# Expert layers: turning X for the router by transposing DMAs in place of TensorE

## The reference

```python
x = x + _L0_ffn_ref(_layernorm(x, axis=-1), L0_ffn_w_router, L0_ffn_w1, L0_ffn_w2, L0_ffn_bias)
# in it, with xf the 2048 tokens x 256 and 8 experts:
scores = jax.nn.softmax(xf @ w_router, axis=-1)
expert_weights, top_experts = jax.lax.top_k(scores, TOP_K)   # TOP_K = 2, capacity 512 per expert
...
x = x + _L1_ffn_ref(_layernorm(x, axis=-1), L1_ffn_W1, L1_ffn_b1, L1_ffn_W2, L1_ffn_b2, L1_ffn_Wr, L1_ffn_br)
# in it:
logits = xf @ Wr + br
topv, _ = lax.top_k(logits, TOPK)
```

## Time and profile before

| | us |
|---|---|
| median of 2 runs | 2664.79 |
| their range | 2664.3 to 2665.28 |
| the profiled execution, span from first to last instruction | 2672.0 |
| what lies outside that span | not listed |

### The profile page before, as it was taken

The page is one execution under the profiler, slowest core; times in us unless marked ns, Lnnn a source line. Parts: engine busy times, 40 slices in busy tenths (PEclk is TensorE's granted clock), DMA queues, the critical chain, the costliest instruction groups (busy, mean ns, idle before and its releaser), DMA issues. The chain is left out here.

```text
span 2672.0 us, 46118 instructions
## 1 busy us (share of the span) xinstructions
PE 2419.7 (91%) x14931; PEld 1416.2 (53%) x15058; DVE 1908.5 (71%) x3499; ACT 1673.2 (63%) x2692; POOL 1804.4 (68%) x1581
## 2 busy tenths in 40 slices
PE   6999999999999999999997588879999999678886
PEld 3555555555555555555553467645444444467665
DVE  7878777787777877777775655468888898764332
ACT  4556756557665566656664555458888788576453
POOL 2677867777777777776768455436878789355553
PEclk9999999999999999999999799989999999699998
DMA  4000000000000000000000744430202020573223
GB/s 144 1 1 1 25 1 1 1 1 5 22 1 1 1 1 1 1 1 1 1 1 15 193 112 116 92 97 18 57 17 58 2 49 1 165 202 72 35 39 60
DMA packets 90917, 107.85 MB, mean 40 GB/s; under 512 B 18867, under 2 KB 80260, under 8 KB 90708
## 3 DMA queue, kind: packets, MB, share of 16 engines
q1 hardware_dynamic: 68500, 80.57, 10.1%
q0 software_dynamic: 21696, 24.98, 6.1%
q10 hardware_dynamic: 544, 0.00, 0.0%
HBM read 68.75 MB, written 25.88 MB: 35 GB/s over the span
## 5 line engine op out<-in xcount | busy, mean ns | idle before, releaser
L417 POOL TENSOR_TENSOR a_acc<-a_acc,a_pf 128x512 f32<-128x512 f32 (+1 forms) x480 | 650.9, 1356 | 312.4 <-ACT a_pf L574 290.7
L574 ACT ACTIVATE a_pf<-a_psS 128x1024 f32<-128x1024 f32 (+1 forms) x288 | 281.5, 977 | 306.1 <-PE a_psS L717 301.8
L869 DVE TENSOR_TENSOR a_pl<-a_pf,a_ph 128x512 f16<-128x512 f32 x448 | 438.2, 988 | 23.2 <-ACT a_ph L580 23.0
L2161 POOL TENSOR_TENSOR c_pl<-c_pf,c_ph 128x512 f16<-128x512 f32 x320 | 374.9, 1199 | 116.9 <-ACT c_ph L2260 116.5
L845 DVE TENSOR_REDUCE a_mx<-a_psA 128x1 f32<-128x512 f32 x504 | 335.3, 683 | 43.7 <-PE a_psA L652 39.6
L580 ACT ACTIVATE a_ph<-a_psS 128x1024 f16<-128x1024 f32 (+1 forms) x288 | 281.5, 977 | 0.0
L1417 POOL DMA_INDIRECT f_sums<-f_xn,f_sidx x78 | 140.5, 1801 | 208.1 <-DVE f_xn L1815 185.6
L1261 DVE TENSOR_TENSOR f_xn<-f_xn 128x256 f16<-128x256 f32 x312 | 130.5, 424 | 197.8 <-ACT f_xn L1230 175.3
L2493 DVE TENSOR_REDUCE c_wf<-c_psA 128x1 f32<-128x512 f32 x384 | 246.5, 681 | 20.1 <-PE c_psA L2332 19.9
L1148 PE MATMUL f_psH<-f_xh,f_w 128*128 128x256 f16 x624 | 173.4, 278 | 83.3 <-ACT f_xn L1230 68.2
L2253 ACT ACTIVATE c_pf<-c_psS 128x1024 f32<-128x1024 f32 x192 | 197.9, 1030 | 67.1 <-PE c_psS L2366 66.0
(11 more groups left out here) (364 smaller groups left out, 6382.0 us busy)
## 6 DMA issues: line engine op xcount, KB each, us to landing
f_stage<-in_L_ffn_w SPq DMA_DIRECT2D x16, 1024.0 KB
f_stage<-in_L_ffn_W SPq DMA_DIRECT2D x16, 1024.0 KB
c_kst<-c_khs SPq DMA_DIRECT2D x64, 100.1 KB, 2.2
a_cx<-in_ctx SPq DMA_DIRECT2D x4, 1536.0 KB
c_cx<-in_ctx SPq DMA_DIRECT2D x12, 512.0 KB, 4.0
f_sums<-X SPq DMA_DIRECT2D x2, 2048.0 KB, 13.2
f_xrow<-f_xn SPq DMA_DIRECT2D x8, 512.0 KB, 4.4
c_kst<-c_kls SPq DMA_DIRECT2D x32, 100.1 KB, 2.2
```

What stands on the lines that cost most here:

```text
L417: g.tensor_tensor(acc[0:k, p, :], acc[0:k, p, :], pf[0:k, q % RF, i, :], ALU.add).then_inc(s_acc, 1)
L574: act.activation(pf[0:r, q % RF, 0:k, :], psS[q % 2][0:r, 0:k, :], ACT.Exp, scale=SCALE).then_inc(s_pF, 1)
L869: v.tensor_tensor(pl[0:r, q % RP, i, :], pf[0:r, q % RF, i, :], ph[0:r, q % RP, i, :], ALU.subtract).then_inc(s_pL, 1)
L2161: g.tensor_tensor(pl[0:r, q % RP, i, :], pf[0:r, q % RF, i, :], ph[0:r, q % RP, i, :], ALU.subtract).then_inc(s_pG, 1)
```

## The change

ScalarE makes the high halves of X in X's own layout, four pieces of 128 x 1024 into `xrh`, and DVE the low halves into `xrl` (`row_low`). Both lie in the space of the weights of expert E - 2. SP then issues eight transposing DMAs, `dma_start_transpose`, each of which turns 128 x 1024 float16 (eight blocks of 128 x 128) into `xth` or `xtl`. In SP's list they stand after the small loads and ahead of the weights of expert 0, of the copies of X and of the rows of `xn`, each behind a wait for its own half. TensorE's transposes of X, ScalarE's and DVE's reads of PSUM and the semaphores between them go. The router's matmuls wait once, for all eight transfers. On DVE the new `row_low` steps take places among the statistics; in layer 1, the branch with `early_stats is None`, the last of them stands ahead of `means(1)`.

```diff
--- before.py
+++ after.py
@@ -953,7 +953,6 @@
              1: ("L1_ffn_Wr", "L1_ffn_W1", "L1_ffn_W2")}[layer]
     GELU = ACT.Gelu_apprx_tanh if layer == 0 else ACT.Gelu
     NQ = NT // 4
-    GI = KC * NQ
     PR = ring(FT, 4)
     HR = ring(FT, 3)
     PIECES = FT
@@ -977,7 +976,8 @@
 
 
         late = w16[:, E - 1, :, :].rearrange("p a f -> p (a f)").bitcast(F32)
-        xth, xtl = w16[:, E - 1, 0:2, :], w16[:, E - 1, 2:4, :]
+        xth, xtl = (w16[:, E - 1, a:a + 2, :].rearrange("p a (t c) -> p (a t) c", c=P) for a in (0, 2))
+        xrh, xrl = (w16[:, E - 2, a:a + 2, :].rearrange("p a f -> p (a f)") for a in (0, 2))
         wb = late.rearrange("p (t c) -> p t c", c=D)
         xn = sb("xn", [P, NT, D])
 
@@ -1050,7 +1050,6 @@
         psH = [ctx.enter_context(nc.psum_tensor(tag + f"psH{i}", [P, 512], F32)) for i in range(3)]
         psX = ctx.enter_context(nc.psum_tensor(tag + "psX", [P, 512], F32))
         psY = [ctx.enter_context(nc.psum_tensor(tag + f"psY{i}", [P, 512], F32)) for i in range(2 * IT)]
-        ring4 = psH + [psX]
         psR = psY[2][:, 0:(NT + 1) * E].rearrange("p (t e) -> p t e", e=E)
         psI = psY[0][:, 0:HI]
         psC = psY[3][:, 0:E]
@@ -1065,9 +1064,9 @@
         s_pool = sem("pool")
         s_rstd = sem("rstd")
         s_nt = sem("nt")
-        s_tP = sem("tP")
-        s_tH = sem("tH")
-        s_tL = sem("tL")
+        s_rowH = sem("rowH")
+        s_rowL = sem("rowL")
+        s_turned = sem("turned")
         s_wr = sem("wr")
         s_cs = sem("cs")
         s_shift = sem("shift")
@@ -1283,6 +1282,13 @@
                 sp.dma_start(bias[:, :], io["L0_ffn_bias"].rearrange("a b d -> (a b) d").to_broadcast([P, D])
                              ).then_inc(s_small, 16)
 
+            for q in range(NQ):
+                cs, ts = slice(4 * q * D, (4 * q + 4) * D), slice(4 * q * KC, (4 * q + 4) * KC)
+                sp.wait_ge(s_rowH, q + 1)
+                sp.dma_start_transpose(xth[:, ts, :], xrh[:, cs]).then_inc(s_turned, 16)
+                sp.wait_ge(s_rowL, q + 1)
+                sp.dma_start_transpose(xtl[:, ts, :], xrl[:, cs]).then_inc(s_turned, 16)
+
             def load_weights(e, half):
 
                 sp.wait_ge(s_wl, (e + 1) * PIECES - PIECES + (half + 1) * PH)
@@ -1463,10 +1469,9 @@
 
             act.wait_ge(s_small, 16 * NSMALL)
             act.activation(wrh[:, :, :], wr[:, :, :], ACT.Copy, scale=WS).then_inc(s_wr, 1)
-            for i in range(GI):
-                kk, q = i % KC, i // KC
-                act.wait_ge(s_tP, i + 1)
-                act.activation(xth[:, kk, q * 512:q * 512 + 512], ring4[i % 4][:, :], ACT.Copy).then_inc(s_tH, 1)
+            for q in range(NQ):
+                act.activation(xrh[:, 4 * q * D:(4 * q + 4) * D], X[:, 4 * q:4 * q + 4, :].rearrange("p t c -> p (t c)"),
+                               ACT.Copy).then_inc(s_rowH, 1)
             def exponentials():
                 act.wait_ge(s_sh, 1)
                 act.activation(ex[:, :, :], sh[:, :, :], ACT.Exp).then_inc(s_ex, 1)
@@ -1522,32 +1527,23 @@
             for L in loops:
                 pe.sem_inc(L.xP, 2)
                 pe.sem_inc(L.hU, FT)
-            for i in range(GI):
-                kk, q = i % KC, i // KC
-                if i >= 4:
-                    pe.wait_ge(s_tL, i - 3)
-                for u in range(4):
-                    ins = pe.transpose(ring4[i % 4][:, u * P:(u + 1) * P], X[:, 4 * q + u, kk * P:(kk + 1) * P],
-                                       identf[:, :])
-                ins.then_inc(s_tP, 1)
             if layer:
                 pe.wait_ge(s_small, 16 * NSMALL)
                 pe.transpose(psY[1][:, 0:E * FT], b1r[:, :], identf[0:E * FT, 0:E * FT]).then_inc(s_b1, 1)
 
 
             pe.wait_ge(s_wr, 2)
-            pe.wait_ge(s_const, 1)
+            pe.wait_ge(s_const, 2)
             for kk in range(KC):
                 for j, w in enumerate((wrh, wrl)):
                     ins = pe.matmul(psC, ones[:, :], w[:, kk, :], start=(kk == 0 and j == 0), stop=(kk == KC - 1 and j == 1))
             ins.then_inc(s_cs, 1)
             for t in range(NT):
-                ts = slice(t * P, (t + 1) * P)
-                if t % 4 == 0:
-                    pe.wait_ge(s_tL, KC * (t // 4) + KC)
+                if t == 0:
+                    pe.wait_ge(s_turned, 2 * NQ * 16)
                 for kk in range(KC):
                     for j, (a, w) in enumerate(((xth, wrh), (xth, wrl), (xtl, wrh))):
-                        ins = pe.matmul(psY[0][:, t * E:(t + 1) * E], a[:, kk, ts], w[:, kk, :],
+                        ins = pe.matmul(psY[0][:, t * E:(t + 1) * E], a[:, t * KC + kk, :], w[:, kk, :],
                                         start=(kk == 0 and j == 0), stop=(kk == KC - 1 and j == 2))
             ins.then_inc(s_lg, 1)
 
@@ -1659,11 +1655,11 @@
                 op(v.scalar_tensor_tensor(shift[:, ts], mv[:, ts, 0], -1.0, rstd[:, ts], ALU.mult, ALU.mult))
                 v.sem_inc(s_shift, 1)
 
-            def turned_low(i):
-                kk, q = i % KC, i // KC
-                cs = slice(q * 512, q * 512 + 512)
-                v.wait_ge(s_tH, i + 1)
-                v.tensor_tensor(xtl[:, kk, cs], ring4[i % 4][:, :], xth[:, kk, cs], ALU.subtract).then_inc(s_tL, 1)
+            def row_low(q):
+                cs = slice(4 * q * D, (4 * q + 4) * D)
+                v.wait_ge(s_rowH, q + 1)
+                v.tensor_tensor(xrl[:, cs], X[:, 4 * q:4 * q + 4, :].rearrange("p t c -> p (t c)"), xrh[:, cs],
+                                ALU.subtract).then_inc(s_rowL, 1)
 
             def split_router():
                 v.wait_ge(s_wr, 1)
@@ -1673,28 +1669,26 @@
             if early_stats is None:
                 stats(range(0, NT // 2))
                 means(0)
-                turned_low(0)
-                turned_low(1)
+                row_low(0)
                 split_router()
                 stats(range(NT // 2, 3 * NT // 4))
                 shifts(0)
-                turned_low(2)
-                turned_low(3)
+                row_low(1)
+                row_low(2)
                 stats(range(3 * NT // 4, NT))
+                row_low(3)
                 means(1)
-                for i in range(4, GI):
-                    turned_low(i)
             else:
                 v.wait_ge(s_early_st, LATE)
                 stats(range(LATE, NT))
                 means(0)
-                turned_low(0)
+                row_low(0)
                 means(1)
-                turned_low(1)
+                row_low(1)
                 split_router()
                 shifts(0)
-                for i in range(2, GI):
-                    turned_low(i)
+                row_low(2)
+                row_low(3)
             shifts(1)
             op(v.tensor_scalar(rstdw[:, :], rstd[:, :], 1.0 / WS, None, ALU.mult))
             v.wait_ge(s_const, 1)
```

## The result

| | before, us | changed, us | ratio |
|---|---|---|---|
| median of 2 runs each | 2664.79 | 2691.04 (2690.14 to 2691.94) | 1.0093 [1.0074, 1.0112] |
| again, 9 and 5 runs on another chip | 2598.96 | 2621.84 (2618.28 to 2623.94) | 1.0083 [1.0070, 1.0097] |
| span of the profiled execution | 2672.0 | 2690.2 (its time 2691.94) | |

The changed kernel is slower, by 26.3 us in the first pair and by 22.9 us in the longer one. 2683 was forecast, 18 us above the median.

What follows compares the result with a forecast made beforehand. TensorE is busy 91% overall, but full DMA bounds the two openings, where data and arithmetic chains meet at L1784. Late bulk 13.3 plus turning 3.4 and 1.3 made 18.0 us: 2683 us, range 2668 to 2722.

Steps and rivals of the forecast that it cites:

- The late bulk: SP's queue, both openings: even with free turning, bulk waits for the last half; L1784 8.0 and 5.3 us late, 13.3 together.
- L1784 waits for the rows of xn: Table build on DVE: waits until xn's rows have left, some 4 us after the arithmetic is ready.
- The price of turning: SP's queue: eight turns end 3.4 us behind the free case in the first opening, 1.3 us in the second.
- t: Time to turn 256 KB on SP's queue: taken as 1.15 us, bounds 0.69 and 5.8 us.
- 8t - 5.8 and 8t - 7.9: Loss in us in first and second opening beyond the 13.3, for t above 1 us.
- the bulk itself: Weights, X's copies and xn's rows on SP's queue: 17.2 us first opening, 17.9 second, at 380 GB/s.
- ScalarE and DVE: Openings: four wide ScalarE copies about 4.2 us, DVE differences 1.2 us each; later shifts(1) covered by the logits.
- TensorE: Openings: removing 32 transposes each gains nothing by itself; the 96 logit matmuls wait for all turns and take 2.5 us.
- Long turning: Rival: transposing occupies SP's queue for long, 53 us (2%) slower at t = 3.4 us, 92 at 5.8; chance 0.13.
- block by block: Rival: each 128x128 block a serial transfer, 122 us per opening, 243 us slower, a time of 2908; chance 0.05.
- The covered bulk: Rival: bulk streams fast enough that L1784 waits for logits alone; 6.2 us slower, 2671; chance 0.12.
- The expert loops: Loops after the table build: unchanged in length.

Runs made afterwards that it cites:

- the repeat: The changed kernel again, no edit, beside the kernel before on another chip: 2621.84 against 2598.96 us.
- before_held: Kernel before with one wait more: weights, copies of X and rows of xn issued only after the last low half; 2613.00 us, 14.0 slower than before.
- after_plain: Changed kernel with plain copies of the same halves in place of the transposing transfers: 2614.84 us, 15.9 slower than before.
- turned_early: As turned_best, with the weights behind the turns instead of ahead: 2675.19 against 2663.97 us for before on its chip.
- weights_first: Changed kernel with the first expert's two weight loads ahead of the transposing transfers on SP's queue: 2614.63 us, 7.2 faster than the changed kernel.
- turned_best: Changed kernel with SP order weights, turns, xn rows, X's copies; high and low halves made ahead of router-weight work: 2613.69 against 2598.44 us for before.
- bulk_first: Changed kernel with weights and both copies of X ahead of the transposing transfers: 2630.95 against 2598.44 us for before.

## Why the prediction was right, and where its sizes were off

*The late bulk, 13.3 us.* Confirmed: holding the bulk back in the kernel before costs 14.0 us. Its parts were each off a little and partly cancel: the weights were issued 11.0 and 13.4 us into the block (12.1 and 13.0 forecast), and from there to the table build it took 20.8 and 21.2 us (20.0 and 20.7). The reading that L1784 waits for the rows of xn is confirmed by 6.22 and 4.79 us of idle time ended by that DMA. I had "some 4 us".

*The price of turning, 4.7 us.* This term was too small. The nearest rows gave t = 1.15 us for 256 KB; the queue shows 1.37. By the prediction's own formula, 8t - 5.8 and 8t - 7.9, the term becomes 5.2 and 3.1, together 8.3 us, and the total 21.6. Measured: 22.9 less 14.0, 8.9 us. That the two agree is in part luck, as the traces of the two openings show.

In the first the weights were forecast for 15.6 us into the block and came at 15.7, because two errors cancel. The turns took 1.8 us longer, but they began 1.7 us earlier: with no weights behind it the bias landed in 3.0 us instead of 4.7, and ScalarE began its copies at 3.6 us into the block instead of 5.4. I had named the bias the slowest transfer that has the queue to itself, and it didn't have it to itself. In the second opening t counts in full, 16.2 us instead of 14.3.

The rest is a term that the sum held constant, the bulk itself. From the weights' first issue to the table build I had 20.0 and 20.7 us; the repeat shows 22.4 and 22.0. The plain copies show 22.0 in both as well, so it isn't the turning, and before_held, with nothing on the queue ahead of the bulk, shows 20.8 and 21.2. Of the repeat's 23.8 us against 18.0, 2.1 are the later issue and 3.7 the longer bulk. What in the bulk takes longer was not tried.

The 261 GB/s of the Trainium skill (DMA: Bandwidth & Descriptors, "Latency and other measured facts") would have given a smaller t still; 0.262 MB in 1.37 us is 191 GB/s, and the window shows 190. Here the measurement decides.

*ScalarE and DVE.* Four high copies took 3.88 us (4.2 forecast), a low half 1.21 to 1.23 us (1.2). `shifts(1)` in the second opening waited 2.17 us for POOL and was covered by the logits, as forecast.

*TensorE.* Taking its transposes away gained nothing: after_plain, without them, loses 15.9 us, and before_held, with them, 14.0. The 96 matmuls took from 1480.65 to 1483.48, 2.8 us, at a clock of 0.50 (2.5 forecast). The logits were forecast for about 1484.1 in a block that begins at 1463.84, 20.3 us into it; they were read 20.5 us into it, by the same two errors that cancel.

*The rivals.* Long turning, over 3.4 us, did not happen, nor block by block: eight blocks take 1.37 us. The page on the three transpose paths (the Trainium skill, VectorE: DVE Perf Modes, "The three transpose paths") prices one block at 1309 ns, and in series that would have been far too dear. The advice of the Trainium skill on the same page ("Rules for kernel authors"), to use TensorE where PSUM will do, agrees with the runs: with turns on an empty queue, turned_early is still 11.2 us behind TensorE. The covered bulk is refuted by before_held. That I found no mechanism for a gain held.

*The expert loops.* They kept their length, as forecast. From the first table build to the second block's first issue it is 794.2 us in both of the first two traces. In the experiments it is 764.4 to 767.6 us on the chips with 2599 us for before and 794.1 to 796.8 us on the one with 2664. From the second table build to the end it is 361.5 us before and 357.8 after, and 313.4 to 317.0 or 350.5 to 351.8 us in the experiments. The spreads, up to 3.7 us, don't follow the delays. The 18.2 us between the first two spans are then 22.7 in the openings, less 3.7 after the second table build and 0.8 ahead of the first block.

## What to carry to other kernels

A transfer placed in front on a queue costs every transfer behind it the wait for its data, also when it is itself cheap: of 23 us here, 14 were idle DMA before bulk traffic that had to move anyway. Find the instruction on which the data chain and the arithmetic chain meet, and count both to it; a step moved off a busy-looking engine gains only if its chain ends last. Here TensorE was idle beside the change, so relieving it gained nothing; whether turning by DMA pays where TensorE or PSUM ends last, no run here shows.

## What the runs showed of the hardware

- A transposing transfer of 128x1024 float16 (256 KB) takes 1.37 us of SP's queue back to back, 190 GB/s with the DMA engines counted as full, and lands 3.3 us after its issue. A plain copy of the same size held the queue for 0.46 to 0.61 us.
- Behind plain traffic on the same queue the first transposing transfer holds the queue far longer, 4.12 us behind 4.5 MB that had been moving for 9 us and 5.66 us behind 2 MB just issued, and the second 1.7 to 2.8 us. Issued 5.2 and 3.0 us after the weights (weights_first), the first took 1.40 and 2.45 us. On an empty queue no transfer was held. The hold ends shortly before the traffic ahead has moved: in turned_best at 1470.64, while 361 GB/s flow until 1472, more than the 190 of turns alone. Plain transfers are held too, but later: behind the same two weight loads a plain copy of 2 MB held the queue for 0.58 to 0.62 us (before, bulk_first), and only the 0.25 MB behind it was held for 7.2 to 7.8 us. What in the queue makes a transfer wait was not tried.
- A turn moves in far more and smaller packets than a plain copy of the same bytes. The pages of before, the changed kernel and after_plain, in this order:

```profile
DMA packets 90917, 107.85 MB, mean 40 GB/s; under 512 B 18867, under 2 KB 80260, under 8 KB 90708
DMA packets 107812, 112.03 MB, mean 42 GB/s; under 512 B 35763, under 2 KB 97156, under 8 KB 107604
DMA packets 93219, 112.03 MB, mean 43 GB/s; under 512 B 19122, under 2 KB 80515, under 8 KB 93011
```

Sixteen turns add 16,895 packets, and the count under 512 B rises by as many (16,896); sixteen plain copies add 2,302.
